# Moving the eight items of keys out of the attention stage's head and into the loop of routed expert tiles

## The reference, cut to what matters

```python
# L0_ffn: every token goes to 2 of 16 experts, and to a shared one
routed = routed + comb[:, e:e + 1] * (silu(g) * u @ experts_down[e])
# L1_xattn: 32 heads of 16 values, 4 x 512 queries, 4 x 512 keys
q = (x @ Wq).reshape(b, n, N_HEADS, HEAD_DIM)        # x: layer norm of the tokens
k, v = split(ctx @ Wkv, 2, axis=-1)                  # ctx: an input
q, k = apply_axial_rope(q, pos), apply_axial_rope(k, pos)
w = softmax(einsum('bqhd,bkhd->bhqk', q, k) * scale)
attn = einsum('bhqk,bkhd->bqhd', w, v).reshape(b, n, 512) @ Wout + bout
```

## Time and profile before

| | |
|---|---|
| median of 3 runs (1582.46 to 1584.0) | 1583.55 us |
| span of the profiled execution | 1581.1 us |
| PE busy | 1453.9 us, 92% |
| DVE busy | 1138.1 us, 72% |
| ACT busy | 974.1 us, 62% |
| POOL busy | 545.9 us, 35% |

### The profile page before, as it was taken

How to read it: one execution, slowest core, us unless ns; L and a number is a source line. 1 busy time by engine, 2 the same in 40 slices (tenths; PEclk the granted TensorE clock), 3 DMA queues, 4 the chain that set the end, 5 groups by cost and what they waited for, 6 DMA issues and landing times. The chain is left out here.

```text
span 1581.1 us, 21473 instructions
## 1 busy us (share of the span) xinstructions
PE 1453.9 (92%) x6233; PEld 633.5 (40%) x6245; DVE 1138.1 (72%) x1660; ACT 974.1 (62%) x1544; POOL 545.9 (35%) x346
## 2 busy tenths in 40 slices
PE   5788988988989999999999798899999999999999
PEld 2344434434444444444444343332333333244444
DVE  7999999999995422222223769899999999637985
ACT  3999999998954011111111542587878878877764
POOL 0689699798971630000003655605000000000000
PEclk7799999999989999999999999999999999999999
DMA  5212314114114484457523725453232332220464
GB/s 188 69 57 86 93 46 115 54 41 120 61 31 178 164 221 160 143 199 264 196 87 127 240 96 164 151 190 91 73 95 73 79 89 72 60 107 14 86 138 123
DMA packets 142519, 183.41 MB, mean 116 GB/s; under 512 B 55491, under 2 KB 89667, under 8 KB 141427
## 3 DMA queue, kind: packets, MB, share of 16 engines
q1 hardware_dynamic: 120918, 134.58, 29.1%
q0 software_dynamic: 6624, 23.14, 4.8%
q10 hardware_dynamic: 14912, 24.89, 4.7%
HBM read 109.29 MB, written 54.92 MB: 104 GB/s over the span
## 5 line engine op out<-in xcount | busy, mean ns | idle before, releaser
L1839 DVE TENSOR_REDUCE a_mx<-a_s 128x2 f32<-128x1024 f32 x256 | 303.3, 1218 | 28.0 <-PE a_s L1955 24.5
L283 POOL TENSOR_TENSOR m_hs<-m_hs,m_C 128x1024 f32<-128x1024 f32 x128 | 301.9, 2385 | 57.4 <-DVE m_hs L508 56.7
L508 DVE TENSOR_TENSOR_SCAN m_hs<-m_dA,m_d 128x512 f32<-128x512 f32 x256 | 294.4, 1200 | 14.8 <-PE m_d L663 12.5
L663 PE MATMUL m_d<-ident_sb,m_dBuT 128*128 128x128 f32 x1024 | 160.1, 289 | 19.7 <-DVE m_hs L508 12.6
L389 ACT ACTIVATE m_dA<-m_dt,m_negA 128x512 f32<-128x512 f32 x256 | 168.0, 712 | 13.7 <-DMA m_dt<-m_dt 12.0
L663 PEld LDWEIGHTS m_d<-ident_sb,m_dBuT 128*128 128x128 f32 x1024 | 116.5, 145 | 145.7 <-DVE m_hs L508 78.6
L1293 PE MATMUL e_gu<-e_w,e_xgT 128*128 x376 | 169.1, 592 | 0.0
L367 ACT ACTIVATE m_dBuT<-m_dtuT,m_BT 128x512 f32<-128x512 f32 x241 | 157.8, 712 | 0.1
L1955 PE MATMUL a_s<-ring_sb 96*128 96x512 bf16 x512 | 150.6, 384 | 5.7 <-DVE a_mx L1839 2.8
L958 ACT ACTIVATE e_sg<-e_gu 128x256 f32<-128x256 f32 x47 | 18.0, 384 | 222.9 <-PE e_gu L1293 222.9
L678 PE MATMUL m_y<-m_hs,m_fold 128*64 128x512 f32 x512 | 142.1, 636 | 3.7 <-POOL m_hs L283 3.7
(11 more groups left out here) (335 smaller groups left out, 2441.6 us busy)
## 6 DMA issues: line engine op xcount, KB each, us to landing
e_w<-in_ex_gu SPq DMA_DIRECT2D x16, 1024.0 KB, 6.6
ring_sb<-qk_dram SPq DMA_DIRECT2D x64, 192.0 KB, 3.1
xg_dram<-zeros_sb SPq DMA_DIRECT2D x47, 256.0 KB, 3.1
e_xg<-xg_dram ACTq DMA_DIRECT2D x47, 256.0 KB, 2.7
yg_dram<-attn_sb ACTq DMA_DIRECT2D x47, 256.0 KB, 2.1
m_C<-c_dram SPq DMA_DIRECT2D x64, 128.0 KB, 2.9
m_dt<-m_dt SPq DMA_DIRECT2D x64, 128.0 KB, 2.4
e_w<-in_ex_dn SPq DMA_DIRECT2D x16, 512.0 KB, 8.5
```

The costliest lines, as they stand in the source:

```text
L283: pool.tensor_tensor(hs[:, J % RH], hs[:, J % RH], C2[:, N % RC].unsqueeze(1).broadcast_to([P, 2, L]), ALU.mult).then_inc(s_hc, 1)
L508: dve.tensor_tensor_scan(hs[:, J % RH, h], dA[:, j % RA], pd[j % RD][:], 0.0, ALU.mult, ALU.add)\
L663: last = pe.transpose(pd[j % RD][:, t * P:(t + 1) * P], dBuT[:, N % 2, t, g], ident[:])
L1839: dve.tensor_reduce(mx[:, r % 2, h * TB + 2 * c:h * TB + 2 * c + 2], psc[c][:], AX.X, ALU.max)\
```

## The change

Four things are done together.

1. `ITEMS` falls from 16 to 8: the head keeps the queries alone. Every item has four matmuls a half, and the items use `pst` and `pvm` in turn as before.
2. The keys are made in the loop of routed tiles. After each of 16 pairs of tiles (pairs 5 to 20, `KEYS_FROM = 5`) PE makes one block of 128 key columns (`key_block`, two matmuls), ACT copies it from PSUM (`copy_key`), and after each second block POOL alone does the rotary turn and the three parts (`key_rows`: eight instructions) and issues the two stores to `qk_dram`. The hardware loops of PE and ACT over pairs become a short loop of single pairs, a loop of four rounds with four pairs written out, and one more pair. POOL waits for the last store before the stage ends.
3. In the head the first three turns of queries (`rotate` 0 to 2) stand between the additions (`combine` 10 to 15), and the turning of x's tiles is spread between the projections.
4. The first maxima (`early_maxes`) stand in another order: those of the later score blocks come after the last turn of queries.

```diff
-            with act.Fori(0, (ST - 5) // 2) as i:
+            def pair(i):
...
+            def copy_key(b, f):
+                act.wait_ge(s_km, b * KD + (f + 1))
+                act.wait_ge(s_kd, b * 2 + (f // 2 + 1))
+                act.activation(raw[:, f // 2, f % 2], pkm, ACT.Copy).then_inc(s_kc, 1)
+
+            with act.Fori(0, KEYS_FROM) as i:
+                pair(i)
+            with act.Fori(0, B) as b:
+                for f in range(KD):
+                    pair(b * KD + (f + KEYS_FROM))
+                    copy_key(b, f)
```

```diff
+            def key_block(b, f):
+                pe.wait_ge(s_kc, b * KD + (f + 1))
+                for k in range(KC):
+                    last = pe.matmul(pkm, kw[:, k, f * P:(f + 1) * P], kctx[:, k, bass.ds(b * L, L)],
+                                     start=(k == 0), stop=(k == KC - 1))
+                last.then_inc(s_km, 1)
+
             pair(0)
-            with pe.Fori(1, (ST - 1) // 2 - 1) as i:
+            with pe.Fori(1, KEYS_FROM) as i:
+                pair(i)
+            pe.wait_ge(s_early, 16 * 4)
+            with pe.Fori(0, B) as b:
+                for f in range(KD):
+                    pair(b * KD + (f + KEYS_FROM))
+                    key_block(b, f)
```

```diff
+            def key_rows(m):
+                b, z = m // 2, raw[:, m % 2]
+                turn = [tab[:, s, b * L:(b + 1) * L].unsqueeze(1).broadcast_to([P, 2, L]) for s in range(2)]
+                pool.wait_ge(s_kc, 2 * m + 3)
+                pool.tensor_tensor(rot, z, turn[0], ALU.mult).then_inc(s_kx, 1)
...
+                pool.tensor_tensor(z, z, turn[1], ALU.mult).then_inc(s_kx, 1)
...
+                pool.tensor_tensor(rot[:, 0], rot[:, 0], z[:, 1], ALU.subtract).then_inc(s_kr, 1)
+                pool.tensor_tensor(rot[:, 1], rot[:, 1], z[:, 0], ALU.add).then_inc(s_kr, 1)
...
+                if m >= 1:
+                    pool.wait_ge(s_kst, 32 * m)
+                pool.tensor_copy(kparts[:, :, 0], rot).then_inc(s_k1, 1)
...
+                pool.tensor_tensor(rot, rot, kparts[:, :, 0], ALU.subtract).then_inc(s_k2, 1)
...
+                pool.tensor_copy(kparts[:, :, 1], rot).then_inc(s_k2, 1)
...
+                pool.tensor_tensor(kparts[:, :, 2], rot, kparts[:, :, 1], ALU.subtract).then_inc(s_k3, 1)
+                pool.sem_inc(s_kd, 1)
```

```diff
-            for t in range(12):
+            def early_maxes(*units):
...
+            for t in range(NT):
                 combine(t)
-                if t % TB == 0 and t >= TB:
-                    inverse(t // TB - 1)
                 if t % TB == TB - 1:
                     variance(t // TB)
...
+                if t in (4, 8, 12):
+                    inverse(t // TB - 1)
+                if t in (9, 11, 13):
+                    rotate((t - 9) // 2)
+            rotate(3)
             inverse(3)
...
+            rotate(4)
+            early_maxes(0)
+            rotate(5)
+            early_maxes(1, 2)
+            rotate(6)
+            early_maxes(3, 4)
+            rotate(7)
+            early_maxes(5, 6, 7)
```

More of the change, by code:

```diff
@@ L750, with moe @@
 GR = 8
[L753 removed]
+KEYS_FROM = 5
+def moe(nc, x_sb, lead, ident, tg, a, xg_dram, yg_dram, s_zero, early, s_early, attn, s_tab, slot, wk, tab_dram, qk_dram, yo, s_yst):
     with ExitStack() as ctx:
@@ L1033, in _ @@
                     store(i * 2 + m, m)
+            def copy_key(b, f):
[8 more added lines that the diff above has]
+                    copy_key(b, f)
+            for i in range(KEYS_FROM + KD * B, (ST - 5) // 2):
+                pair(i)
             for j in range(ST - 3, ST):
@@ L1602, in _ @@
                              vout[:, b % RV].rearrange("p g k c -> p g (k c)")).then_inc(s_vs[b % RV], 16)
+            store(0)
             sp.wait_ge(s_cmb, 3 * NT)
             sp.dma_start(ones_row, a["ones"]).then_inc(s_one, 16)
[L1605 to L1612, removed]
+            sp.wait_ge(s_ps[0], 32)
+            for r in range(RG):
                 load_qk(0, r)
-            for n in range(4, FIRST + 5):
+            for n in range(1, 5):
                 store(n)
@@ L1622, in _ @@
             load_v(0, 1)
-            for n in range(FIRST + 5, ITEMS - 2):
-                store(n)
+            store(5)
             maxima(0, 1)
@@ L1672, in part_3 @@
                     .then_inc(s_p3, 1)
-            for n in range(2):
-                rest_1(n)
-                part_3(n)
+            rest_1(0)
+            part_3(0)
+            inverse_root(3)
+            rest_1(1)
+            part_3(1)
             rest_1(2)
@@ L1938, in project @@
                         pe.wait_ge(s_qr, 2 * n - 2)
-                    if n % 4 == 0:
+                    if n % 2 == 0:
                         pe.wait_ge(s_xtc, TB * (b + 1))
-                for k in range(kn):
-                    last = pe.matmul(pair_bank(n)[:, c], w[:, k, f:f + P], src[:, k, b * L:(b + 1) * L],
-                                     start=(k == 0), stop=(k == kn - 1))
+                for k in range(KD):
+                    last = pe.matmul(pair_bank(n)[:, c], wq[:, k, f:f + P], xnT[:, k, b * L:(b + 1) * L],
+                                     start=(k == 0), stop=(k == KD - 1))
                 last.then_inc(s_qm, 1)
@@ L2025, in step, with early_scores @@
                         turn_values(i, r - 1)
+            def early_scores(*parts):
+                for u, c in parts:
+                    scores(0, u // G4, u % G4, c)
             pe.wait_ge(s_early, 16 * 4)
```

178 lines of the change are left out of this document (103 added, 75 removed).

## The result

The changed kernel takes **1568.05 us** (median of 4 runs, 1563.26 to 1568.44), the kernel before 1583.49 beside it (1582.46 to 1584.0): ratio 0.990, 95% interval 0.9885 to 0.9915, that is 15 us less. The forecast was 1572 in 1564 to 1581. The profiled execution took 1568.37 us with a span of 1566.5.

A forecast was written before the change was run, and what follows sets the result against it. PE bounds the routed loop; the head has no single bound, PE and DVE being nearly full in its middle. +27.5 - 36.4 - 2.4 = -11.3 us, so 1583.55 falls to 1572 us, range 1564 to 1581.

The forecast's parts named there:

- +27.5 in the loop: Routed loop: 16 key blocks of 1.72 us on nearly full PE lengthen it by 27.5 us.
- seams (4.8): Routed loop: upper bound of 4.8 us if each of 16 seams cost PE 0.3 us more than its matmuls.
- the last item (4.7): Routed loop's end: POOL's last key item charged 0, with +4.7 us as upper end if it outlasts PE.
- my bounds of 1.26 to 3.16: POOL's key chain: a cast of 128x1024, shown in no row, bounded between 1.26 and 3.16 us.
- my 15.9 to 19.7: POOL's key chain in the routed loop: 15.9 to 19.7 us per item, items coming every 26.7 us.
- -36.4 in the head: Head: new order counted from PE's start at 853.35 to a main loop start at 973.2, 36.4 us less.
- the steps of the count: Head, by row durations: values end 885.5, PE projects to 934.9, first score ready 935.6, DVE then bounds to 970.1.
- (d): Head, two corrections on 970.1: +2.1 us old-order shortfall, some 1.0 for additions blocked by POOL; main loop starts 973.2.
- The 1.0 for blocked additions: Head: additions 12 and 13 stand still beside POOL, up to 4.2 us on DVE, some 1.0 on PE.
- -2.4 at the main loop's start: Main loop's start, term (e): PE's 2.42 us wait for item 15's last turn goes, giving -2.4 us.
- a bound of the sum (-2.1 to +3): Whole sum: clock in PE's new pauses of 4 to 5 us near the head's end could push it -2.1 to +3.
- the head gives back little more than PE's share: Rival, chance 0.09: head returns PE's 31.2 us and the 2.4 wait but not DVE's share; -6, 1578 to 1584.

The follow-up runs named there:

- the two pairs: Two profiles each of the kernel before and the changed kernel, the second taken later on another chip: spans 1581.1 and 1566.5 us, then 1577.5 and 1564.9.
- With the clock kept up: Changed kernel plus nine groups of unread matmuls in PE's pauses at the head's end; ratios 0.9871 and 0.9909 on two chips, main loop 384.96 us in the second profile.

## Why the prediction was right

**+27.5 in the loop: +26.5 and +27.6 in the two pairs.** PE's record of 1.72 us a block was the whole cost, as the kernel without the blocks shows (27.3). The bounds for seams (4.8) and for the last item (4.7) were not used: DVE's product (`e_hm`) took 421 ns in both kernels' loops, and POOL had issued its last store 9.5 us before PE's last product ended. The cast, which no row of before had, took 1.04 us and was outside my bounds of 1.26 to 3.16; the products with the table took 2.34, above the 2.12 to 2.16 that I had put. The errors nearly cancel: 15.8 us an item, just under my 15.9 to 19.7. The Trainium skill (GPSIMD Engine Reference, Engine selection) has GpSimd at roughly line rate for one input and about 2 times slower than VectorE for two. By it I had put a cast near half of a two-input instruction; here it is 1.04 against 2.13, so the trace agrees, and it was the better bound.

**-36.4 in the head: -38.7 and -43.0.** Told from PE's start at the barrier (876.37 here, 853.35 there, so 23.02 is taken off), the steps of the count were: item 0 starts at 885.5, measured 885.2; first maximum 935.6, measured 936.2; start of the main loop 970.1 before the corrections, 970.9 measured. The term that was mis-sized is (d), the 3.1 us put on top, where 0.8 were needed. The 2.1 us by which the count had fallen short in the old order were that order's: its turned tiles stood behind pauses of PE, at half clock, and the new order has neither there (PE without a pause above 0.83 us from 908 to 976, its eight turns at 1.04 each time). The 1.0 for blocked additions was right in kind: the two instructions of addition 12 took 3.60 us, those of 13 took 1.53. But PE's only wait for a query turn behind them was 0.43 us (at 948.93), and DVE had 4.81 us to spare at the first maximum, so it cost next to nothing. The first split was slow (3.4 us, 3.3 forecast), the second 0.7 (0.75). The Trainium skill (SBUF — State Buffer, Who interferes with whom) covers the additions and the split's `a_mr`: a DVE instruction with two SBUF inputs contends with a GpSimd instruction that reads SBUF. The rows agree, 3.60 beside a POOL instruction at 928.05 against 1.53, but the blocked time is only a cost where DVE has no wait behind it. My wording in (d), two SBUF inputs, was too narrow for my own rows: the split's cast has one input and took 2.05 beside POOL.

The second pair's -43.0 is no better forecast of mine: both heads moved from one profile to the next, by 2.4 and 1.9 us.

**-2.4 at the main loop's start: +0.9 and +0.4.** This term failed, with the wrong sign. The wait for item 15's turn did go, as said. But PE paused for 4.00 and 3.29 us at the new head's end, the clock was at half until some 10 us into the main loop, and PE's next wait was for ACT's exponential. I had that clock as a bound of the sum (-2.1 to +3) and not in this term. Followed from the first score pair, PE turns the first results (`a_aT`) 59.9 us later in the changed kernel against 60.1 before, in the second pair 59.8 against 59.7: the start gave 0.2 and nothing, not 2.4. With the clock kept up that point came at 58.1 us, 1.6 to 2.0 us ahead of the kernel before; that this stage ended 2.7 us shorter, near the 2.4 that I had counted, is partly chance. The loss that turns the sign lies 62 us in, where I had not looked: PE waits 1.80 and 1.61 us for a load from `qk_dram`, and 0 and 0.66 in the two profiles of the kernel before. All eleven profiles with the change have a wait of 1.2 to 2.1 us ahead of that pair of scores (in three of them DVE's maxima come last, in the others the load); what makes it was not tested.

**The sum.** -11.3 forecast; behind the first routed product -11.1 in the first pair and -14.9 in the second. The whole times say -15.4 and about -17 (1.1% of 1581), each 2.4 more or less. That the first pair's sum is so near is luck: the head came 2.3 us and the loop 1.0 better than forecast, the main loop 3.3 worse. What stays open is some 2 to 4 us between the stages' mean (-13.0) and the medians' (-16): the start's scatter of 6 us from one execution to another is large enough for it, but two profiles of each kernel cannot tell a small steady gain there from chance.

**Where the gain comes from.** Not from the moved keys alone: with the old order no gain can be told (0.9997, 0.9974 to 1.0021). Of the head's 38.7 us some 23 come with the keys and 16 with the order, and nearly all of those 16 with its first half: turned tiles spread between projections, and three query turns between additions, so that PE runs through its projections with no pause above 0.83 us. What the order would give with the keys still in the head no run shows, so the gain belongs to the two together, and its split between them is known from one side only. The rival "the head gives back little more than PE's share" is nearly what the old order does, and is worth less still: 23 to 25 us came back, less than PE's own 31.2.

## What to carry to other kernels

Work moved onto an engine that is full costs its length there (27.3 us for 27.5 of records); what it frees is only gained if the stage that it leaves is put in a new order so that its engines close the gap. Count such a stage forward by row durations from one event, and do not carry an old order's shortfall over to a new one: pauses and the low clock behind them belong to an order. A blocked or slow instruction is charged only where nothing behind it on its engine waits anyway. And a pause that the new order leaves at a stage's end is charged to the next stage: look there for the clock, and for the wait that comes next when one is taken away.

## What the runs showed of the hardware

- POOL: a cast of 128x1024 took 1.04 us, a two-input instruction with one float32 and one bfloat16 input 2.13, and the products of keys and table 2.34; these have two float32 inputs, and the table is read twice over, and no run tells which of the two costs the 0.2.
- DVE: in the changed kernel `a_nmr`, on 128x4 values, took 0.14 us at 909.91 and 2.00 at 948.80, beside POOL; a query turn's first product, with a PSUM operand, took 1.22 with or without POOL.
- TensorE: after pauses of 4.00 and 3.29 us the same four matmuls took 2.17 us for 1.03, and the main loop's records were back at full clock (0.60 a pair) from 1004 on, PE having been busy from 993.3 on but for 0.36 and 1.76 us.
- The same kernel on the same kind of chip reached its loop at 567.8 and at 574.0 us; on one of the three chips of the experiments the kernel before took 12 to 14 us longer than on the others.
